# Three query, key and output projections as sums of high and low parts, and a new order of scores and maxima

## What is computed

```python
x = x + attn(cond(x, lang), Wq, Wk, Wv, Wf, bf)          # part one, for each of the 16 sequences
x = x + ffn(cond2(x, expert))                            # parts two and three
# cond: u = x + W2[lang]^T relu(W1[lang]^T x + b1) + b2; layer norm; gamma, beta -> norm
# attn: q = norm Wq^T (16 heads of 16), k = norm Wk^T, v = norm Wv^T (one head, shared)
#       softmax(q k^T / 4, causal) v  -> att;   att Wf^T + bf
```

## Time and profile before

| | |
|---|---|
| median of 3 runs | 1118.78 us (1117.38 to 1119.62) |
| the profiled execution | 1118.38 us, of which its span (first to last instruction) is 1116.4 us |
| PE busy | 1093.7 us (98%) |
| DVE busy | 785.6 us (70%) |
| ACT busy | 586.6 us (53%) |
| POOL busy | 173.9 us (16%) |
| granted TensorE clock | full in all 40 slices |

### The profile page before, as it was taken

One profiled execution on the slowest core, in us unless ns is written; L12 is line 12 of the kernel. 1 busy time (PEld: TensorE's weight loads), 2 busy tenths in 40 slices (PEclk: granted clock), 3 DMA queues, 4 the chain that ended last, 5 costly groups with the idle time before them and its releaser, 6 DMA issues.

```text
span 1116.4 us, 18106 instructions
## 1 busy us (share of the span) xinstructions
PE 1093.7 (98%) x5979; PEld 862.5 (77%) x5995; DVE 785.6 (70%) x1378; ACT 586.6 (53%) x988; POOL 173.9 (16%) x192
## 2 busy tenths in 40 slices
PE   7899999999989999999999999999999999999998
PEld 4577677776757888888888888888888888888886
DVE  3867777777787557755688765888748777577875
ACT  2456566565656444532556564655636565455653
POOL 2122223222353543431000000000000000000000
PEclk9999999999999999999999999999999999999999
DMA  7445656557745655645134531245421454304421
GB/s 173 81 89 117 110 123 114 113 115 162 230 118 188 225 177 206 215 164 208 38 132 151 170 132 56 96 149 169 151 75 44 163 169 151 113 11 140 150 94 39
DMA packets 82255, 148.57 MB, mean 133 GB/s; under 512 B 15504, under 2 KB 42016, under 8 KB 82080
## 3 DMA queue, kind: packets, MB, share of 16 engines
q1 hardware_dynamic: 72690, 126.92, 40.1%
q10 hardware_dynamic: 9518, 21.11, 5.3%
HBM read 107.63 MB, written 30.41 MB: 124 GB/s over the span
## 4 chain that ended last, share of the span: by engine, by line
PE 93%; DVE 3%; DMA 1%; ACT 1%; issue 1%; SPq 1%; POOL 0%; ACTq 0%; DVEq 0%; POOLq 0%
PE bank L1720 36%; PE bank L1682 11%; PE bank L1434 7%; PE bank L1732 5%; PE bank L1352 4%; PE bank L1658 4%; PE bank L1652 4%; PE bank L1371 3%; PE bank L1318 3%; PE bank L1390 3%; PE bank L1426 2%; PE bank L1355 2%; PE bank L1286 1%; PE bank L1298 1%; PE bank L1410 1%; DMA q_t<-q_high 1%
## 5 line engine op out<-in xcount | busy, mean ns | idle before, releaser
L1720 PE MATMUL bank<-op_hi,w_ring 128*128 128x512 f32 x896 | 348.6, 389 | 0.0
L1720 PE MATMUL bank<-op_lo,w_ring 128*128 128x512 f32 x896 | 348.6, 389 | 0.0
L1179 DVE TENSOR_TENSOR op_lo<-x_blk,op_hi 128x512 fp32r<-128x512 f32 x288 | 193.7, 684 | 30.4 <-ACT op_hi L839 30.3
L839 ACT ACTIVATE op_hi<-x_blk 128x512 fp32r<-128x512 f32 x288 | 162.8, 620 | 73.5 <-PE bank L1720 69.3
L1720 PEld LDWEIGHTS bank<-op_hi,w_ring 128*128 128x128 f32 x896 | 168.2, 188 | 35.1
L1720 PEld LDWEIGHTS bank<-op_lo,w_ring 128*128 128x128 f32 x896 | 168.1, 188 | 34.9
L962 DVE TENSOR_REDUCE neg_max<-bank 128x2 f32<-128x512 f32 (+1 forms) x192 | 124.7, 685 | 32.4 <-PE bank L1355 30.3
L646 ACT ACTIVATE p<-bank 128x512 f32<-128x512 f32 x192 | 108.9, 596 | 37.9 <-PE bank L1371 33.6
L863 ACT ACTIVATE x_blk<-x_blk,scales 128x512 f32<-128x512 f32 x96 | 69.3, 722 | 67.0 <-DVE x_blk L1232 28.9
L1682 PE MATMUL bank<-tile_hi,ffn_w 128*128 128x512 f32 x256 | 101.6, 397 | 0.0
L541 POOL TENSOR_SCALAR_AFFINE_SELECT p<-p 128x512 f32<-128x512 f32 (+1 forms) x96 | 76.2, 794 | 158.8 <-ACT p L646 158.7
(11 more groups left out here) (127 smaller groups left out, 1731.5 us busy)
## 6 DMA issues: line engine op xcount, KB each, us to landing
w_ring<-hid_scratch SPq DMA_DIRECT2D x112, 512.0 KB, 4.6
hid_scratch<-comb ACTq DMA_DIRECT2D x8, 1792.0 KB, 7.8
q_t<-q_high SPq DMA_DIRECT2D x64, 128.0 KB, 4.7
comb<-in_hid_d ACTq DMA_DIRECT2D x6, 768.0 KB, 4.9
xt<-in_x_t SPq DMA_DIRECT2D x16, 256.0 KB, 3.4
xtok<-in_x_tok SPq DMA_DIRECT2D x16, 256.0 KB
resid<-in_x_t SPq DMA_DIRECT2D x16, 256.0 KB, 3.0
q_t<-q_rest SPq DMA_DIRECT2D x32, 128.0 KB, 4.5
```

Source lines behind the costliest of these rows:

```text
L839: nc.scalar.activation(op_hi[:, o % OP_RING, k], x_blk[:, operand_home(o), k], ACT.Copy).then_inc(s["op_hi"], 1)
L1179: nc.vector.tensor_tensor(op_lo[:, o % OP_RING, k], x_blk[:, operand_home(o), k], op_hi[:, o % OP_RING, k].bitcast(F32), ALU.subtract).the ...
L1720: last = mm(banks[first_bank + m][:, :], w, read(v[:, q % OP_RING, k, :]), start=k == 0 and v is op_hi and i not in (P2, P3), stop=k == KB ...
```

## The change

The six weight blocks and the two inputs of the projections are split. `x_high` is x rounded to fp32r, `x_low` is x - x_high, also as fp32r, and a product becomes high·high + low·high + high·low, three fp32r matmuls for one fp32 matmul, added up in PSUM. Four things come with that:

- the weights: loaded into raw buffers and split on DVE in `split_queries_weights`, `split_keys_weights` (before the first sequence) and `split_out_weights` (end of iteration 0, where PE waits for it before its loop);
- the inputs: ACT rounds `norm_t` (`norm_parts`), DVE subtracts (`norm_rest`) in each iteration; ACT's copy `att_t` is now the rounded one and DVE subtracts it from PSUM (`attention_low`);
- the waits: `project_queries` waits for `norm_hi` and, for its last third, for `norm_low`; `project_out` for `att_low`; `adapter_out` and `products_transposed` for `att_low` where they waited for `att_t_out`;
- the orders of PE, DVE, ACT and SP in whole iterations and in iterations 14 (and, for SP, the loads).

```diff
+            def norm_parts(n):
+                act.wait_ge(s["norm_t_out"], n + 1)
...
+                nc.scalar.activation(norm_high[:, :, :], norm_t[:, :, :], ACT.Copy).then_inc(s["norm_hi"], 1)
...
+            def norm_rest(n):
+                dve.wait_ge(s["norm_hi"], n + 1)
+                nc.vector.tensor_tensor(norm_low, norm_t[:, :, :], norm_high[:, :, :].bitcast(F32), ALU.subtract).then_inc(s["norm_low"], 1)
+
+            def attention_low(b):
+                dve.wait_ge(s["att_t_out"], b + 1)
+                nc.vector.tensor_tensor(att_low, side[1][:, :].rearrange("p (k t) -> p k t", k=KD), att_t[:, :, :].bitcast(F32),
+                                        ALU.subtract).then_inc(s["att_low"], 1)
...
+            def split_out_weights():
+                dve.wait_ge(s["out_loaded"], 32)
+                nc.vector.tensor_copy(wf_high, wf_raw).then_inc(s["wf_hi"], 1)
+                dve.wait_ge(s["wf_hi"], 1)
+                nc.vector.tensor_tensor(wf[:, :, :], wf_raw, wf_high.bitcast(F32), ALU.subtract).then_inc(s["weights_split"], 1)
...
             def project_queries(n, tail):
-                pe.wait_ge(s["norm_t_out"], n + 1)
+                pe.wait_ge(s["norm_hi"], n + 1)
...
+                for w in (wq_high, wq):
+                    for m in range(KD):
+                        for k in range(KD):
+                            mm(ring[0][:, m * T:(m + 1) * T], w[:, k, m * P:(m + 1) * P], norm_high[:, k, :], start=w is wq_high and m == 0 and k == 0, stop=False)
+                pe.wait_ge(s["norm_low"], n + 1)
                 for m in range(KD):
                     for k in range(KD):
-                        last = mm(ring[0][:, m * T:(m + 1) * T], wq[:, k, m * P:(m + 1) * P], norm_t[:, k, :], start=k == 0, stop=k == KD - 1)
+                        last = mm(ring[0][:, m * T:(m + 1) * T], wq_high[:, k, m * P:(m + 1) * P], norm_low[:, k, :], start=False, stop=m == KD - 1 and k == KD - 1)
...
+                pe.wait_ge(s["att_low"], b + 1)
...
-                        last = mm(side[0][:, m * T:(m + 1) * T], wf[:, k, m * P:(m + 1) * P], att_t[:, k, :], start=k == 0, stop=k == KD - 1)
+                        last = mm(side[0][:, m * T:(m + 1) * T], wf_high[:, k, m * P:(m + 1) * P], att_low[:, k, :], start=False, stop=m == KD - 1 and k == KD - 1)
...
-                    pe.wait_ge(s["out_loaded"], 32)
+                    pe.wait_ge(s["weights_split"], 3)
...
+            split_queries_weights()
             normalise(0)
+            split_keys_weights()
+            norm_rest(0)
...
+                load_rest(b + 3, l)
                 load_inputs(b + 3, l)
-                load_rest(b + 3, l)
                 move_queries(b + 2, (slot + 2) % SLOTS)
-                store_x1(b - 1)
                 move_maxima(b + 1, (slot + 1) % SLOTS)
                 load_resid(b)
+                store_x1(b - 1)
                 copy_ffn(b - 1)
```

More of the change, by code:

```diff
@@ L139, in build @@
         xa_hi, xa_lo = yc_hi[:, 0], yc_lo[:, 0]
+        wq_high, wf_high = yc_hi[:, 1, :, 0:D], yc_hi[:, 1, :, D:2 * D]
+        norm_low, att_low = yc_lo[:, 1, :, 0:T], yc_lo[:, 1, :, T:2 * T]
         before_ring = ExitStack()
@@ L617, in affine @@
                 act.wait_ge(s["norm_t_mm"], n + 1)
+                if not is_first(n):
+                    act.wait_ge(s["norm_low"], n)
                 for k in range(KD):
@@ L668, in iteration @@
                     affine(b + 2)
+                    norm_parts(b + 2)
                     queries_high(b + 2)
@@ L767, in _ @@
             affine(0)
+            norm_parts(0)
             act.wait_ge(s["const_loaded"], 80)
@@ L1002, in iteration @@
                     maximum(b + 1, 0)
+                    norm_rest(b + 2)
                     maximum(b + 1, 1)
@@ L1056, in iteration @@
                     maximum(b + 1, 3)
+                    maximum(b + 1, 4)
                 if tail:
@@ L1061, in iteration @@
                     split_fc2a()
+                if front:
+                    norm_rest(b + 2)
                 if maxima:
-                    maximum(b + 1, 4)
                     maximum(b + 1, 5)
                     maximum(b + 1, 6)
+                    maximum(b + 1, 7)
                 if front:
@@ L1068, in iteration @@
                 if maxima:
-                    maximum(b + 1, 7)
                     maximum(b + 1, 8)
                     maximum(b + 1, 9)
+                if tail:
+                    attention_low(b - 1)
+                if maxima:
                     maximum(b + 1, 10)
@@ L1141, in cond2_tile @@
                 for m in range(KH):
+                    if is_first(t) and m == 5:
+                        attention_low(B - 1)
                     dve.wait_ge(s["raw_ready"], KH * t + m + 1)
@@ L1326, in project_keys @@
                     pe.wait_ge(s["values_out"], 2 * n)
-                for k in range(KD):
-                    last = mm(ring[1][:, 0:T], wkv[:, k, :], norm_t[:, k, :], start=k == 0, stop=k == KD - 1)
+                if is_first(n):
+                    pe.wait_ge(s["weights_split"], 2)
+                passes = [(w, v, k) for w, v in ((wkv_high, norm_high), (wkv, norm_high), (wkv_high, norm_low)) for k in range(KD)]
+                for i, (w, v, k) in enumerate(passes):
+                    last = mm(ring[1][:, 0:T], w[:, k, :], v[:, k, :], start=i == 0, stop=i == len(passes) - 1)
                 last.then_inc(s["kv_mm"], 1)
@@ L1541, in iteration @@
                     products(b - 1, behind, True, maxima)
+                if softmax:
+                    scores(b, slot, 0)
                 if maxima:
@@ L1544, in iteration @@
                     max_scores(b + 1, ahead, 1)
-                if tail:
-                    products_transposed(b - 1, 0, front)
-                if softmax:
-                    scores(b, slot, 0)
-                if maxima:
-                    max_scores(b + 1, ahead, 2)
                 if softmax:
@@ L1566, in iteration @@
                     max_scores(b + 1, ahead, 4)
+                    max_scores(b + 1, ahead, 5)
                 if softmax:
@@ L1573, in iteration @@
                 if maxima:
-                    max_scores(b + 1, ahead, 6)
-                if softmax:
-                    scores(b, slot, 6)
-                if maxima:
                     max_scores(b + 1, ahead, 7)
-                if front:
-                    project_keys(b + 2, tail)
-                if softmax:
-                    scores(b, slot, 7)
+                if tail:
+                    attention_transposed(b - 1)
                 if maxima:
@@ L1585, in iteration @@
                 if softmax:
-                    scores(b, slot, 8)
+                    scores(b, slot, 6)
+                    scores(b, slot, 7)
                 if maxima:
                     max_scores(b + 1, ahead, 9)
-                if tail:
-                    attention_transposed(b - 1)
+                if front:
+                    project_keys(b + 2, tail)
+                if maxima:
+                    max_scores(b + 1, ahead, 10)
                 if softmax:
+                    scores(b, slot, 8)
                     scores(b, slot, 9)
                 if maxima:
-                    max_scores(b + 1, ahead, 10)
                     max_scores(b + 1, ahead, 11)
@@ L1604, in iteration @@
                     scores(b, slot, 11)
+                if maxima:
+                    maxima_transposed(b + 1)
+                if front:
+                    values_transposed(b + 2)
             pe.wait_ge(s["warm_made"], 1)
```

71 lines of the change are left out of this document (45 added, 26 removed).

## The result

The changed kernel takes 1128.18 us (median of 6 runs, 1126.57 to 1132.39), the kernel before 1118.99 in the same session: a ratio of 1.0083 (95% interval 1.0067 to 1.0100). It is 0.83% **slower**, clear of the noise, and outside the predicted range. The profiled execution took 1126.57 us with a span of 1124.6, so 8.2 us more than the 1116.4 of before are to be found.

The account below looks back on a forecast made before the run. DVE's chain was to set the period at 19.2 us, with PE following. Twelve iterations saving 0.5 each (6.0), 3.2 lost at the beginning and 0.1 saved at the end gave -2.9: 1115.9 us, range 1110.5 to 1119.5.

Parts of the forecast that it names:

- What PE saves: The three projections of each iteration, split into fp32r products, fall from 4.32 to 3.54 us on PE, 0.78 saved.
- VectorE's chain sets the period: In each loop iteration, DVE's chain from the first maximum to `add_residual` sets a period of 19.2 us, 0.5 less.
- it gives 0.2 back: At each iteration's end, subtraction L978 comes 0.3 later in POOL's mask, so it takes 0.2 us less (0 to 0.37).
- The maxima late: Rival, chance 0.11: `scores` 0 waits for moved maxima each iteration; at +5.9 the period is 20.1, total 1126.6 us.
- PE keeps its saving: Rival, chance 0.2: in the loop gaps close and POOL is not met; period 18.7, total 1109.9 us.
- It cancels: Rival, chance 0.2: each new handover in the loop costs 0.1 more; period 19.45, total within 0.2 us of before.
- The beginning: Before the loop nothing is saved and four added costs sum to 3.4 us, taken as 3.2.
- (a): In iteration 0 PE waits for `split_out_weights`, a cast and subtraction behind `keys_low` on DVE: 1.9 us late.
- (b): In iteration 0 the output weights' subtraction falls together with POOL's last mask and waits: 0.8 us (0 to 0.9).
- (c): In iteration 0 ACT's rounding delays `q_high`, for which DVE idles, less what PE saves: 0.3 us.
- (d): Before the first sequence, `split_queries_weights` ahead of `normalise` and rounding behind it move first queries 0.4 us later (0.2 to 1.0).
- The end: Iteration 14 waits away what 13 gains; DVE's added work and shorter `project_out` in 14 and 15 together save 0.1 us.

Follow-up runs that it names:

- e6: The changed kernel with all engine orders of the kernel before put back, projections still split: 1134.53 us, 1.0129 of the kernel before.
- e5: The kernel before with the change's orders alone, projections full fp32 and nothing split: 1127.90 us, 1.0087 of the kernel before.
- e4: The changed kernel with GpSimd's mask of score unit 4 held until VectorE has split the maxima: 1129.32 us, 1.0089 of the kernel before.
- e9: The changed kernel with the edits of e7 and the mask edit of e4: 1116.28 us, 0.9966 of the kernel before.
- e1: The changed kernel with TensorE's wait for `weights_split` 3 moved from iteration 0's end to the head of `project_out`: 1124.83 us, 1.0057 of the kernel before.
- e3: The changed kernel with the edits of e1 and e2 and six more `keep_warm` loads ahead of iteration 0: 1119.58 us, 1.0014 of the kernel before.
- e7: e3 with the 3 MB `ffn_w` load issued behind the small moves on SyncE's queue: 1117.56 us, 0.9979 of the kernel before.
- e2: The changed kernel with `attention_low` ahead of `check_first_chunk` and behind `split_fc2a` on VectorE in iteration 15: 1125.05 us, 1.0045 of the kernel before.
- e10: The kernel before with only the 3 MB `ffn_w` load issued behind the last moves of queries and maxima: 1119.22 us, 0.9993 of the kernel before.

## Why the prediction was wrong

- **What PE saves**: 0.78 was forecast, and TensorE's busy time fell by 0.49 (19.61 - 19.12 in the windows). Both numbers of "from 4.32 to 3.54" were off. The first took `project_out`'s 0.432 for all ten products. From start to start the query projection took 126.34 - 124.70 = 1.64 and that of the keys 128.15 - 127.47 = 0.68, which with `project_out`'s 1.73 makes 4.05. The kernel before:

```profile
126.34 0.58 PE L1352 MATMUL bank<-keys,q_t 128*128 128x512 f32 x1
127.47 1.03 PE L1328 MATMUL bank<-norm_t,wkv 128*128 128x256 f32 x4
128.15 0.58 PE L1371 MATMUL bank<-q_t,keys 128*128 128x512 f32 x1
```

The second took 0.118 for each of the thirty. They take 1.53 + 0.80 + 1.49 = 3.82, 0.127 each. The row I took it from the earlier trace rows has products in a long run of their kind; here they come in groups of 2 to 4, and the first pass of a group takes longer (0.58 for the first pass of four, 0.47 for the next). The changed kernel:

```profile
132.50 0.74 PE L1381 MATMUL bank<-norm_high,tile_hi 128*128 128x256 f32 x4
133.08 0.64 PE L1381 MATMUL bank<-norm_high,wq 128*128 128x256 f32 x4
133.55 0.64 PE L1385 MATMUL bank<-tile_lo,tile_hi 128*128 128x256 f32 x4
134.03 0.40 PE L1422 MATMUL bank<-keys,q_t 128*128 128x512 f32 x1
136.08 0.49 PE L1398 MATMUL bank<-norm_high,wkv_high 128*128 128x256 f32 x2
136.88 0.39 PE L1422 MATMUL bank<-keys,q_t 128*128 128x512 f32 x1
137.98 0.72 PE L1497 MATMUL bank<-att_t,tile_hi 128*128 128x256 f32 x4
139.47 0.63 PE L1441 MATMUL bank<-q_t,keys 128*128 128x512 f32 x2
```

  So the projections themselves save 0.23, and the rest of the 0.49 lies in the score and maxima units between them. How much the split saves depends on what stands around it: 0.25 of busy time in the old order (e6), 0.69 in the new one (e5).

- **VectorE's chain sets the period**: right for the changed kernel, and the walk was close. Maximum 0 came at +6.01 (forecast +5.98), one short gap was there (0.27 ahead of unit 4, forecast 0.2), and `norm_rest` and `attention_low` took 0.60 each on the chain, as forecast, without TensorE waiting for them.

```profile
127.32 1.29 DVE L1010 TENSOR_REDUCE neg_max<-bank 128x4 f32<-128x512 f32 x2 [0.25 <-remote]
...
131.35 0.69 DVE L1010 TENSOR_REDUCE neg_max<-bank 128x2 f32<-128x512 f32 x1 [0.27 <-PE bank L1425]
```

  The term that failed is "it gives 0.2 back", said of L978: the mask met the cast one operation earlier, and the pair took 0.60 + 0.19 where it took 0.18 + 0.56 before. e4 and e9, where the cast takes 0.18 again, show that it was the mask, and that this was worth only 0.12 of the 0.42, since TensorE's smaller saving was waiting behind it. The 0.15 for `normalise` in the first mask did not come (L956 takes 0.74 at 129.15, beside a mask from 128.78 to 129.42, and L935 0.73 before, beside none). What is left of the 0.28 between 19.2 and 19.48 is spread over the chain. TensorE idled 0.36 per iteration (19.48 - 19.12), 0.29 of it at `adapter_in`, and not 0.9.
- **The maxima late**, my rival on the slower side: no. No steady iteration waits for a transfer at `scores` 0.
- **The other rivals**: "PE keeps its saving" fell with the two terms above, the saving and L978. "It cancels" had a period of 19.45, nearly the one measured, but by handovers that cost more each; they didn't, and with 3.2 for the beginning it would still have come out even.
- **The beginning**: 6.26 in place of 3.2. From one start of `adapter_in` to the next it is 0.49 at the very first (6.19 against 5.70; the twelve profiled executions lie between 5.48 and 6.19), 0.70 up to iteration -1, 1.34 in it and 3.73 in iteration 0. The last is mostly (a) and (b): without the wait for `weights_split` 3, in e1, iteration 0 takes 3.41 less, where (a) and (b) had 2.7. The subtraction met the mask just as (b) said (1.46 in place of 0.69). (c) was right in size: without that wait iteration 0 takes 0.32 more than before, though it has waits of 1.62 for the moved maxima (1.02 before) and of 0.64 for `norm_high`. (d) had 0.4 for the 0.70. The Trainium skill ("SBUF — State Buffer", Who interferes with whom) has it that an operation of VectorE with two inputs in SBUF and one of GpSimd that reads SBUF exclude each other; the 1.46 against 0.69 agrees. What was missing altogether is the half clock: one stretch at 27, and one at 62. The first costs 1.3: iteration -1 takes 21.2 to 21.3 in the three split kernels that have it (changed, e4, e6) and 20.0 to 20.1 in the six that don't. With the second, iteration 1 took 1.6 more than a steady one. The runs with the new order and no half clock there take 0.6 to 1.2 more (e1, e3, e7, e9), so the clock's part is between 0.4 and 1.1; why iteration 1 takes 0.6 more without it stays open.
- **The end**: "I count 0.1 for both" is the step that failed most plainly: 3.1 were lost there in place of 0.1 saved. I looked at the units of TensorE in iteration 15 and not at what stands ahead of `attention_low` in VectorE's order there: the old wait had been on ACT's `att_t_out` alone, the new one is on VectorE, which was busy for 6 us with work for part two. e2 and e3 show it (3.7 with its half clock; without wait and half clock this part takes 781.8, 0.6 less than the kernel before, which is why 3.1 and not 3.7 are lost). That iteration 14 eats what 13 gains held in the changed kernel (42.4 in both); in the versions that arrive there earlier it ate 1.9 to 6.0, until e7, for the reason given there.

The sum of the misses: 3.1 at the beginning, 4.8 in the loop (235.5 us measured, 236.7 - 6.0 forecast; 1.9 of it is iteration 1, the rest the eleven others), 3.2 at the end; from -2.9 that gives the 8.2 that were measured. The loop is the largest of the three. Twelve iterations at the steady 19.48 would gain 2.8 us and not 6.0, which is less than the 3.2 forecast for the beginning: even with both ends as forecast the kernel would not have become faster.

That the half clock follows the long waits is borne out by e1, e2 and e3: where they took a wait away, the stretch behind it went too. Over the nine profiled executions with split products it is the same: the four that wait for the split weights (3.17 to 3.64 us: changed, e2, e4, e6) have a stretch at 60 to 62 and the five others none, and the four that wait for `attention_low` in iteration 15 (2.36 to 2.38: changed, e1, e4, e6) have one that begins within 1.5 us of its end, and the five others none. What makes one wait bring it and another not stays open. It came after 3.47 and 4.83 us in iteration 14 (e2, e4) and after 1.29 and 1.39 close together, and it did not after 2.87 (e1, iteration 14), 2.78 (e5) or after 1.29 and 1.32 (e2, near 26); e9 and e10 have one near 40, behind a wait of 1.23, where other executions have none. The rival that the lighter products bring it by themselves is not borne out: e3 and e7 have the same products and none, and e10 has one with full fp32.

## What to carry to other kernels

- When a product is split into high and low parts, follow the new low operand through every iteration, the first and the last above all: its wait goes to another engine, and what that engine does there at the ends (here loads, splits and checks for the next part) is in front of it.
- A wait of two or three microseconds of TensorE can cost more behind it than its own length: 1.3 us more behind the 2.36 of iteration 15. Look at the granted clock in windows of a few microseconds; the page's line of tenths read 9 in every slice here. And put a wait where the operand is read, not at the end of a stage.
- Order and arithmetic don't add: in a steady iteration here each alone lost and both together won, while the two ends lost more than that. Test them together and apart.

## What the runs showed of the hardware

- A 128x32 cast of VectorE beside a running mask of GpSimd takes 0.60 in place of 0.18, until the mask ends. It has a single input in SBUF; I had looked for such meetings only at operations with two.
- One large transfer under way (3 MB, landing 11 to 16 us after issue) held back the moves issued behind it on the same queue. Moves of 128 KB landed 4.4 us after issue without it and up to 8.4 with it (e4), latest where they followed it most closely. TensorE then waited 0.81, 1.93, 2.87, 3.47 and 4.83 us for the moved maxima (8 KB each) in five kernels, and 0.97 and 0.99 with the load behind them (e9, e7).
- Four fp32r products of 256 columns took 0.58 us as the first pass of a projection and 0.47 as the next; 0.47 is also their price in a long run (three took 0.35).
